# Adding the last two expert steps by one-hot matmuls, and part of the final sum on GpSimd

## The reference

```python
logits = hidden_states @ router_w + router_b
probs = jax.nn.softmax(logits, axis=-1)
topw, topi = jax.lax.top_k(probs, K)                  # K = 4 of E = 16
topw = topw / jnp.sum(topw, axis=-1, keepdims=True)
...
def body(acc, expert):
    w1e, b1e, w2e, b2e, ce = expert
    hmid = jax.nn.gelu(x @ w1e + b1e, approximate=False)
    return (acc + (hmid @ w2e + b2e) * ce[:, None], None)
...
x = _layernorm(x + _L0_ffn_ref(x, ...), axis=-1)
```

## Time and profile before

| what | us |
|---|---|
| median of 3 runs | 586.83 |
| lowest, highest | 585.78, 587.88 |
| the profiled execution | 587.42 |
| its span, first to last instruction | 585.6 |
| TensorE matmul busy | 546.6 (93%) |
| VectorE busy | 399.3 (68%) |
| ScalarE busy | 321.6 (55%) |
| GpSimd busy | 269.9 (46%) |

### The profile page before, as it was taken

One profiled execution on the slowest core, in us unless ns is written; L12 is line 12 of the kernel. 1 busy time (PEld: TensorE's weight loads), 2 busy tenths in 40 slices (PEclk: granted clock), 3 DMA queues, 4 the chain that ended last, 5 costly groups with the idle time before them and its releaser, 6 DMA issues.

```text
span 585.6 us, 14223 instructions
## 1 busy us (share of the span) xinstructions
PE 546.6 (93%) x4048; PEld 505.4 (86%) x4048; DVE 399.3 (68%) x898; ACT 321.6 (55%) x658; POOL 269.9 (46%) x255
## 2 busy tenths in 40 slices
PE   5999999999998989989789999999999999999774
PEld 4988998888987978878678899999999999999752
DVE  2636656656567747778334598878789779878754
ACT  2424333333345535554355678777778767977505
POOL 6650000000013646555636545576576575557713
PEclk9999999999998979989979999999999999999988
DMA  8699999980000312323848989999999999999494
GB/s 271 227 385 385 385 385 386 386 290 0 1 1 22 106 73 82 116 81 118 271 141 252 293 229 271 269 258 247 263 252 252 263 259 243 263 254 237 55 279 157
DMA packets 91558, 127.49 MB, mean 218 GB/s; under 512 B 6708, under 2 KB 62708, under 8 KB 91528
## 3 DMA queue, kind: packets, MB, share of 16 engines
q1 hardware_dynamic: 76328, 107.23, 55.1%
q0 software_dynamic: 14304, 19.67, 16.5%
q10 hardware_dynamic: 896, 0.23, 0.2%
HBM read 62.59 MB, written 64.52 MB: 217 GB/s over the span
## 4 chain that ended last, share of the span: by engine, by line
PE 63%; issue 12%; DMA 9%; DVE 5%; ACT 4%; another core or an unknown queue 2%; POOL 2%; ACTq 1%; POOLq 0%; DVEq 0%; SPq 0%
PE ps L395 12%; PE ps L397 11%; PE ps L396 11%; DMA expert_sum<-yb,home_row 8%; PE ps L970 3%; PE ps L897 3%; PE ps L1092 2%; PE ps L1078 2%; PE ps L933 2%; PE ps L962 2%; PE ps L954 2%; PE ps L1014 1%; PE ps L1219 1%; PE ps L1018 1%
## 5 line engine op out<-in xcount | busy, mean ns | idle before, releaser
L704 POOL DMA_INDIRECT expert_sum<-yb,home_row x76 | 150.3, 1977 | 88.0 <-DVE home_row L1931 49.6
L395 PE MATMUL ps<-gT_h,w_h 128*128 128x256 f32 x288 | 83.6, 290 | 1.3 <-issue 1.3
L395 PE MATMUL ps<-w_h,h_h 128*128 128x256 f32 x288 | 81.6, 283 | 1.9 <-DVE h_l L1917 1.6
L397 PE MATMUL ps<-w_h,h_l 128*128 128x256 f32 x288 | 81.4, 283 | 0.0
L396 PE MATMUL ps<-w_l,h_h 128*128 128x256 f32 x288 | 81.3, 282 | 0.0
L397 PE MATMUL ps<-gT_h,w_l 128*128 128x256 f32 x288 | 80.6, 280 | 0.0
L396 PE MATMUL ps<-gT_l,w_h 128*128 128x256 f32 x288 | 80.5, 280 | 0.0
L650 POOL DMA_INDIRECT expert_rows<-x_all,idx x64 | 63.2, 987 | 34.4 <-issue 29.9
L634 POOL TENSOR_TENSOR rstd<-ve,mhalf 128x1 f32<-128x1 f32 x16 | 8.8, 553 | 116.3 <-DVE ve L1650 116.3
L1917 DVE TENSOR_TENSOR h_l<-hf,h_h 128x1024 fp32r<-128x1024 f32 x35 | 42.9, 1225 | 23.8 <-ACT h_h L1489 17.0
L1482 ACT ACTIVATE hf<-ps,b1s 128x256 f32<-128x256 f32 x140 | 55.1, 489 | 5.2 <-PE ps L397 5.1
(11 more groups left out here) (300 smaller groups left out, 1414.0 us busy)
## 6 DMA issues: line engine op xcount, KB each, us to landing
expert_rows<-zeros SPq DMA_DIRECT2D x32, 1152.0 KB, 14.3
w1f<-in_L_ffn_w SPq DMA_DIRECT2D x40, 512.0 KB
w2f<-in_L_ffn_w SPq DMA_DIRECT2D x40, 512.0 KB
xg<-expert_rows SPq DMA_DIRECT2D x40, 288.0 KB
expert_sum<-zeros SPq DMA_DIRECT2D x10, 256.0 KB, 9.9
x_all<-in_x SPq DMA_DIRECT2D x8, 256.0 KB, 7.2
expert_sum<-x_all SPq DMA_DIRECT2D x8, 256.0 KB
total<-expert_sum SPq DMA_DIRECT2D x4, 512.0 KB, 5.8
```

What stands on the lines that cost most here:

```text
L395: pe.matmul(o, ah, bh, start=first, stop=False)
L397: return pe.matmul(o, al, bh, start=False, stop=last)
L704: pool.indirect_dma_start(out=sums[p], out_offset=bass.IndirectOffsetOnAxis(ap=home_row1[:, t, c:c + 1] if early else home_row[:, p, c:c + ...
```

## The change

- **Step L-1 is no longer stored.** It is treated like step L: `y_split` and the new `rest_of_y` split it into `y2_h` and `y2_l`, `choose` makes a second one-hot matrix `chosen2`, and TensorE adds it with eight more matmuls for each pair of tiles. `results_halved`, `y_out_halved` and the use of `home_rows` for it are gone. `chosen2` takes the place in SBUF in which `ot` is written later; `y2_h` and `y2_l` that of `yb1`.
- **A table.** `tokens` (128 x 2048, token numbers, the same in every partition) is built in `total2` by four additions of 128x512 on VectorE, one behind `h_low` in each of steps 5 to 8. `choose(p, c)` compares it with the row's token number in one TENSOR_SCALAR. The first runs at `home_further` of L-1, the others behind that of L.
- **The loads.** `sums[0]` is loaded once L-3 is stored, in the order `IN_TURN` = 0, 1, 4, 5, 2, 3, 6, 7; then `sums[1]`, once L-2 is stored and the four `choose` are done, since `tokens` lies in `total2`.
- **The final sum.** For the first six pairs of `IN_TURN` GpSimd adds `total2` to `total` in SBUF (`both_sums`), three ahead of its first power and one behind each of the next three, and VectorE adds the sum to the bank. For the last two TensorE adds `total` by the identity and VectorE adds `total2`. VectorE's addition to the bank now stands inside its loop, behind TensorE's last matmul of the pair.

The core of the diff:

```diff
@@ sync
+            for c in range(2):
+                sp.wait_ge(st_y[0][c], more * 16 + 16 * (PAIRS_LEAST - 1))
+            for m in IN_TURN:
+                load_even(m)
             for c in range(2):
                 sp.wait_ge(st_y[1][c], more * 16 + 16 * (PAIRS_LEAST - 1))
-            for m in range(NT // 4):
+            sp.wait_ge(tb_dve, TABLE_STEPS + 8)
+            for m in (i // 2 for i in IN_TURN[::2]):
                 sp.dma_start(total2[:, 4 * m:4 * m + 4], ...).then_inc(odd_in[m], 16)
-            for c in range(2):
-                sp.wait_ge(st_y[0][c], more * 16 + 16 * PAIRS_LEAST)
-            for m in range(NT // 2):
-                load_even(m)
@@ gpsimd
+            def both_sums(i):
+                m = IN_TURN[i]
+                pool.wait_ge(pair_in[m], 32)
+                pool.wait_ge(odd_in[m // 2], 16)
+                pool.tensor_tensor(total[:, 2 * m:2 * m + 2], total[:, 2 * m:2 * m + 2], total2[:, 2 * m:2 * m + 2], ALU.add).then_inc(sum_ok, 1)
@@ tensor
             bias_sums(0)
-            pe.wait_ge(yok, more * 2 + (2 * PAIRS_LEAST - 1 + BIAS))
+            pe.wait_ge(tb_dve, TABLE_STEPS + 6)
             pe.wait_ge(yll, 2)
+            for m in IN_TURN[:2]:
+                add_chosen(m, 0)
+            pe.wait_ge(yll, 4)
             bias_sums(1)
...
+            for i, m in enumerate(IN_TURN):
+                if i >= 2:
+                    add_chosen(m, 0)
+                mm = add_chosen(m, 1, i < POOLED)
+                if i >= POOLED:
+                    mm = add_even(m)
+                mm.then_inc(pe_sum, 1)
@@ vector
+            def choose(p, c):
+                dve.wait_ge(tb_dve, TABLE_STEPS + 4)
+                dve.tensor_scalar(chosen_by(p, c), tokens, home[:, p, c, E:E + 1], None, ALU.is_equal).then_inc(tb_dve, 1)
...
+            def last_further(t, p, k):
+                home_further(t, p, k)
+                choose(1 - p, 1)
+                rest_of_y(t - 1, 1 - p)
+                for c in range(2):
+                    choose(p, c)
+                rest_of_y(t, p)
...
+            for i, m in enumerate(IN_TURN):
+                dve.wait_ge(pe_sum, i + 1)
+                if i < POOLED:
+                    dve.wait_ge(sum_ok, i + 1)
+                    left = total
+                else:
+                    dve.wait_ge(odd_in[m // 2], 16)
+                    left = total2
+                dve.tensor_tensor(ps[:, m], ps[:, m], left[:, 2 * m:2 * m + 2]..., ALU.add).then_inc(odd_ok, 1)
```

More of the change, by code:

```diff
@@ L399, in decoder_layer, with chosen_by @@
         f = lambda ap: ap.bitcast(F32)
+        last_y = [(y2_h, y2_l), (y_h, y_l)]
+        tokens = total2[:].rearrange("p a d -> p (a d)")[:, 0:TOKENS].rearrange("p (t c) -> p t c", c=P)
+        def chosen_by(p, c):
+            return chosen[:, c] if p else chosen2[:, :, c]
         def router_of(kc):
@@ L1004, in bias_sums @@
                         m = i // 2 * (NT // 4) + half * 2 + i % 2
-                        mm = pe.matmul(ps[:, m, a * D:(a + 1) * D], shT[rows, half * 2 + a], b2s[rows], start=a == 0, stop=False, skip_group_check=True)
-                mm.then_inc(eb, 1)
+                        pe.matmul(ps[:, m, a * D:(a + 1) * D], shT[rows, half * 2 + a], b2s[rows], start=a == 0, stop=False, skip_group_check=True)
             def project(t, p, k):
@@ L1450, in y_out @@
                 ins.then_inc(yok, 1)
-            def y_out_halved(t, p, k):
-                expert = act.value_load(tab[1:2, ds(t, 1)], min_val=0, max_val=E - 1)
-                act.wait_ge(yps, done(t))
-                act.wait_ge(hmon, done(t))
-                for c in range(2):
-                    act.wait_ge(st_y[p][c], 16 * k)
-                act.sem_inc(passed, 1)
-                for c in range(2):
-                    act.activation(yb[:, p, c], ps[:, 6 + p, c * D:(c + 1) * D], ACT.Copy,
-                                   scale=home_on[:, p, c, ds(expert, 1)]).then_inc(yok_part if c == 0 else yok, 1)
             def g_high(t, p, k):
@@ L1518, in _ @@
             pipeline_upto(act, more, [(3, y_out), (0, g_high), (1, w2_high), (1, gelus), (1, h_high)],
-                          closing={(y_out, 2): y_out_halved, (y_out, 1): y_split, (gelus, 1): gelus_halved, (h_high, 1): no_high})
-            for m in range(NT // 2):
-                act.wait_ge(shift_ok, m + 1)
+                          closing={(y_out, 2): y_split, (y_out, 1): y_split, (gelus, 1): gelus_halved, (h_high, 1): no_high})
+            for i, m in enumerate(IN_TURN):
+                act.wait_ge(shift_ok, i + 1)
                 for a in range(2):
                     act.activation(ot[:, 2 * m + a], ps[:, m, a * D:(a + 1) * D], ACT.Identity,
-                                   bias=shift[:, m % 2, a:a + 1], scale=trstd[:, m % 2, a:a + 1]).then_inc(eo, 1)
+                                   bias=shift[:, i % 2, a:a + 1], scale=trstd[:, i % 2, a:a + 1]).then_inc(eo, 1)
         @block.vector
```

129 lines of the change are left out of this document (61 added, 68 removed).

## The result

The changed kernel takes 587.62 us (median of 20 runs, 582.01 to 591.87); the kernel before, beside it, 583.65 (20 runs, 579.56 to 588.40). The ratio is 1.0058, 95% interval 1.0037 to 1.0079: **slower by 3.4 us**. The medians themselves lie 4.0 us apart; the ratio leaves out two runs of the changed kernel that took over 1.5% more than its fastest. The forecast was no change at 586.8; the time lies in the range of the prediction (584.3 to 588.9), the direction was wrong. The three runs that the prediction started from (586.83) lay 3.2 us above the median of twenty, so the predicted time is nearer to 587.62 than the predicted difference, 0, is to 3.4.

The account below looks back on a forecast made before the run. It took the chain through L-1's store, then TensorE's pace in the even additions, as the bound. Removing that store gave -2.0 us, GpSimd's hold on VectorE +2.0, sum 0.0: 586.8 us, range 584.3 to 588.9.

Parts of the forecast that it names:

- the table's: Steps 5 to 8 of the loop: four VectorE additions hidden, cost nothing; up to 2.8 us if the cover were gone.
- the four table operations lie on the path: Rival, steps 5 to 8 of the loop: the additions cost 2.8 us, end at 589.6; chance 0.04.
- no new wait on TensorE: Sign, expert loop: the changed kernel's timeline shows no new TensorE wait between 335 and 550 us.
- Choosing: VectorE's four choose operations near the loop's end: 1.27 us each, the last ending at 556.3.
- The rival of 2.25 us: Between home_on and the odd loads: choosing at one element a cycle, 2.25 us each, end at 589.0; chance 0.12.
- The gate of the odd loads: Ahead of the odd loads: L-2's store, 7.4 us beside the even loads, decides at 557.15, after the choose at 556.3.
- if the odd loads go out before 556 or after 558.5: Sign, odd loads' issue, expected at about 557: outside these times the prediction calls itself wrong.
- First landing: Odd loads: the first 512 KB land 3.9 us after their issue, at 561.05.
- The hold: Final sum: GpSimd's sums delay VectorE's shift, 1.0 us in pair 2, 0.5 each in pairs 3 and 4, together 2.0.
- Tail as a whole: End of the kernel: last tve 2.0 us earlier, the hold takes back 2.0 us, no change.

Follow-up runs that it names:

- a_again: The changed kernel, unchanged, measured once more: 1.0069 of the kernel before.
- a_pefirst: The changed kernel with TensorE's two pairs first instead of last and GpSimd's six sums for the third to eighth pair: 1.0066 of the kernel before.
- b_table: The kernel before with only the four 128x512 additions on VectorE in steps 5 to 8, result unused: 1.0042 of the kernel before.
- b_ahead8: The kernel before with all eight pairs' one-hot additions ahead of the first even one (AHEAD 8 instead of 5): 1.0104 of the kernel before, six runs.
- b_again: The kernel before, unchanged, measured once more: 1.0012 of the kernel before.
- b_table_again: The kernel before with the four unused additions in steps 5 to 8, a second time: 1.0026 of the kernel before.
- b_tgap: The kernel before with the same four unused additions, placed in VectorE's wait ahead of the loop: 1.0009 of the kernel before.
- a_split2: Second run of: changed kernel, table ahead of loop, TensorE adding first and last two pairs, four even loads behind odd ones: 0.9975 of the kernel before.

## Why the prediction was wrong

- **The step that failed is the table's.** "I cost them at nothing: between 335 and 550 us TensorE waits 1.6 us for VectorE's h_l, four times, so VectorE runs ahead of it nearly everywhere." The row is right, the conclusion isn't. A wait total says that the lead was gone four times, not how large it is in the other steps. The term was 0; it measured 2.0 to 2.3 us in excess, near the upper bound of 2.8 that stood beside it. The rival "the four table operations lie on the path", with a chance of 0.04, came true in size, though by another way: with four of them under 0.1 us is lost in steps 5 to 8 themselves, and the rest at steps without a lead, from 11 to the end of the loop. The four waits of the earlier trace rows themselves were the sign. The prediction also looked for this loss in the wrong place: "no new wait on TensorE" is what the waits view shows, while the excess is 2.8 us.
- **Choosing:** taken at 1.27 us, measured 1.28 alone and 2.47 for two. The 1227 ns of the Trainium skill (VectorE: DVE Perf Modes, The perf-mode tier table) agree with the 2.47 us for two. The rival of 2.25 us is out, also for the two that write every second block.
- **The gate of the odd loads:** predicted the store (7.4 us) over the choose. In the changed kernel's three profiles the choose decided twice (ended at 555.47 and 555.40, issues at 555.55 and 555.49) and the store once (a_again, 1.5 us later, 7.7 behind its second half). The issue was predicted at 557.15; by the prediction's own sign, "if the odd loads go out before 556 or after 558.5", this step failed in all three profiles (558.76 in a_again, where step L also began 1.0 us later). The store's 7.4 us were right where it decided and too long where it had landed within 7.0.
- **First landing:** taken at 3.9 us, measured 4.95 from the issue to the start of GpSimd's sum. Off by 1.0 us; the gate, 1.6 us earlier than predicted, made up for it.
- **The hold:** predicted 2.0 us in three pairs, measured 1.2 (pitches 2.63 + 2.14 + 2.11 - 3 x 1.89). The end of each shift follows the end of the sum, as forecast; the first held shift cost 0.7 us (2.63 - 1.89) and not 1.0, the next two 0.25 and 0.22 and not 0.5 each. The tve of the first pair takes 0.61 us in the changed kernel and 1.05 in a_pefirst, instead of 0.17. By the Trainium skill (SBUF — State Buffer, Who interferes with whom) a tensor_scalar in a two-port mode is held by GpSimd as well; no row of before showed it, these do.
- **Tail as a whole:** predicted -2.0 + 2.0 = 0; the means of six profiles each differ by -0.3 us. This half of the forecast was right, in part by luck: in the first profile the last tve comes 1.2 us earlier than forecast, 0.8 of it from the shorter hold, and the mean comes out since before's first tail was 0.5 us above before's mean and the store gated some of the others.
- **The clock** is missing in the working. In before TensorE stands idle for 2.4 us ahead of the even additions, and the granted clock then is at its 1.2 GHz level just where TensorE sets the pace. TensorE's busy time, granted clock, DMA share and GB/s by stretches of 2 us, before:

```profile
564.00:566.00 2.00, 0.00 (x0) 1.00 0.71 193
566.00:568.00 2.00, 1.71 (x3) 0.68 0.94 221
568.00:570.00 2.00, 2.00 (x5) 0.50 1.05 360
```

  In b_table the same 3.4 us came at 558.4, while TensorE did one-hot additions ahead of need, and the tail is 47.1 instead of 49.3. All seven profiles with the tail of before have one or two such stretches of 3.4 us in it ahead of TensorE's last matmul; the twelve with the changed one have none, and TensorE has no pause over 0.3 us there (in before two of 2.4 us). That the pauses bring the slow stretch fits this; only b_ahead8, which took the second pause away, varied them. The 1.72 us for four identity matmuls is a row at 2.4 GHz; the first four, in the slow stretch, took 3.41 us in before and 1.98 in b_table. The tails follow: 49.1 to 49.8 us in the four profiles with the slow stretch at the even additions (before, b_again, b_table_again, b_tgap), 47.1, 47.6 and 48.2 in the three where it fell earlier. So whether the changed tail is shorter or longer than before's depends on which execution is compared.
- **What stays open:** the twenty runs say 3.4 us, excess and tail together 2.3 - 0.3 = 2.0 (1.7 with the fit). The rest is within the errors of both (standard errors of 0.6 and 0.7 us), and no run tied it to a place.

## What to carry to other kernels

Before work is put on an engine "that runs ahead", measure its lead step by step (end of its product to first use) at the start, in the middle and at the end of the loop; a total of waits says nothing of the steps in which the lead just sufficed. When a one-time job has to be done, put it where that engine waits for data, as here the 4.8 us ahead of the loop, where the four additions took 2.5 us and delayed nothing. And where one execution differs from the next by more than the change is worth, cut it into stretches with a fixed pitch and compare these.

## What the runs showed of the hardware

- A GpSimd TENSOR_TENSOR of 128x512 in SBUF makes VectorE's smallest SBUF operations wait until its own end, within 0.03 us: a TENSOR_SCALAR of two elements a partition took 1.05 us instead of 0.17, a SCALAR_TENSOR_TENSOR 1.24 instead of 0.13. VectorE's additions into PSUM (0.69 to 0.70) and its statistics (0.76) beside the same sums did not change.
- The second indirect DMA of a store, with 2 MB of loads beside it, was waited for 7.1 to 7.9 us in the five profiles of the changed tail where it decided, and 7.2 to 8.6 in before's tail (7.44 in before, 8.43 in b_again); in five others of the changed tail it had landed within 7.0. With 1 MB beside it, it had landed within 6.25 us (a_split2, 527.98 to 534.23).
- A wait of TensorE for an operand is shown some 0.25 us shorter than the step it lengthens: in before 0.25, 0.44 and 0.20 us where the steps took 0.50, 0.70 and 0.45 over 6.13.
- One of the chips ran the kernel before in 565.67 us, the others in 581.16 to 585.54. Excess and tail are like elsewhere on it (0.0 to 4.2 and 46.4 to 49.8 us); the 17 us are gone ahead of step 7, whose transposes start at 318.4 to 319.1 us instead of 328.8 to 340.8.
